# Four-bit feed-forward: Pool's passes over h in quarters of 176 columns, VectorE's sum into the output in one pass over both tiles

## The chip, the cores and the metric

The kernel runs on one core of a Trainium2 chip. The metric is the device time of one execution in microseconds (us), read as the median of the runs; smaller is better. The core has TensorE (matrix products, PE in the profile; its weight loads are PEld), VectorE (DVE), ScalarE (ACT), GpSimd (POOL, called Pool below) and SyncE (SP, which here issues the loads and stores). Each engine works through its own list of instructions in order; they meet through semaphores.

## The reference

A batch of 2 x 2048 rows of 256 numbers goes through four blocks, each added to x behind a layer normalisation: an agent attention, a transformer layer with sixteen heads and eight experts, a selective scan, and a feed-forward whose operands are rounded to four bits. Only the last block is touched:

```python
def fp4_quant_dequant(x):                       # blocks of 16 along the last axis
    scale = jnp.max(jnp.abs(xb), axis=-1, keepdims=True) / 6.0
    scale = jnp.maximum(scale, jnp.float32(1e-12))
    xn = xb / scale
    idx = jnp.searchsorted(_MID, jnp.abs(xn))
    q = _GRID[idx] * jnp.sign(xn) * scale
gate = fp4_linear(x, w_gate)                    # 256 -> 704, x and w both rounded
y = fp4_linear(x, w_up)
h = jax.nn.silu(gate) * y
return fp4_linear(h, w_down)                    # 704 -> 256, h rounded too
x = x + _layernorm(that)
```

## The kernel before, in words

The 4096 rows are 32 tiles of 128 rows (128 partitions); `fp4_ffn` takes two tiles at a time (UT = 2), so 16 units. A unit passes through stages that lie on five engines. `run_stages` writes each engine's list: in step s the engine does, in the order given, its stages, each for the unit s - behind. The order of the work of an engine is thus fixed by hand, and semaphores alone tie the engines together.

What happens to a unit u: TensorE projects (`project`, into ps_p), VectorE adds xm and takes the statistics (`add_xm`), ScalarE normalises into z, VectorE makes x3 (`make_x3`), ScalarE normalises x3 into xf, VectorE rounds xf to four bits (`make_x`, lines 2389 to 2408), Pool takes the rounding constant off again and multiplies by the scale (`scale_x`, L2732 and L2736, into xq). TensorE turns xq (`turn_x`, L2841), ScalarE and VectorE split it in a high and a low part (`copy_x` L2761, `split_xq` L205), and TensorE makes gate and up in 18 products a tile (`gate_up`, L2850). ScalarE brings them into gate, up and sig (`take_gu`), Pool multiplies up by gate (`times_up`, L2715), ScalarE finishes the sigmoid, and Pool multiplies by it into h (`times_sigmoid`, L2725; h is 2 x 704 = 1408 columns a partition). VectorE rounds h (`make_h`): the maximum of each block (L2389), its scale (L2391), the inverse (L2393), the product (L2402), two operations that build the rounding constant (L2404, L2406) and the sum with it (L2408). Pool subtracts the constant (`scale_h`, L2744) and multiplies by the scale into hq (L2750). TensorE turns hq (`turn_h`, L2859) and multiplies by the down weights (`down`, L2867), VectorE takes the statistics (`stats_out`), ScalarE normalises into v (`scale_out`), VectorE adds x3 into o (`make_out`, L2703), and SyncE stores it.

Pool's order in a step: `times_sigmoid` of the unit s - 3, `scale_h` of s - 4, `scale_x` of s - 1, `times_up` of s - 2. Each of the four passes over h goes over two tiles in two halves of 352 columns, so it is four instructions. The x passes are two instructions of 256 columns each.

VectorE's order: `stats_out`, `add_xm`, `stats_x3`, `variances`, `split_xq`, `scales` (four operations on six numbers a partition, L2665 to L2671, called the tiny operations below), `make_h` of s - 4, `make_x3`, `make_x`, `make_out`.

Semaphores that matter: `gu_product` counts the pieces of `times_up`, and `times_sigmoid` waits until all of its unit are there; `gu_used` rises once behind the last piece of `times_sigmoid`, and VectorE's `make_h` waits for it; `h_rounded` rises when L2408 is done and starts the subtraction; `hq_steps` counts the subtracted pieces; `hq_turned` (TensorE) lets Pool write hq again; `hq_ready` rises once behind the last scaled piece; `out_ready` counts finished tiles of the output, for SyncE's store and ScalarE's `scale_out`.

Of the kernel before, what the change touches and what calls it, by code (L numbers as in the profile page):

```python
# [16 lines left out]
ALU = mybir.AluOpType  # L17
# [135 lines left out]
def run_stages(eng, units, *stages, unroll=False, ways=2):  # L153

    stages = [(stage, behind, own[0] if own else units) for stage, behind, *own in stages]

    def step(s, way):
        for stage, behind, count in stages:  # L160
            if not isinstance(s, int) or 0 <= s - behind < count:
                stage(s - behind, (way - behind) % ways)

    starts, ends = [behind for _, behind, _ in stages], [behind + count for _, behind, count in stages]
    if unroll:
        for s in range(min(starts), max(ends)):
            step(s, s % ways)
        return

    first, last = -(-max(starts) // ways) * ways, min(ends) // ways * ways  # L170
    for s in range(min(starts), first):
        step(s, s % ways)
    with eng.Fori(first // ways, last // ways) as i:
        for way in range(ways):
            step(i * ways + way, way)
    for s in range(last, max(ends)):
        step(s, s % ways)


def third_on(unit):  # L180

    return not isinstance(unit, int) or unit >= 2
# [6 lines left out]
def over(ap, shape):  # L189

    return ap.broadcast_to(shape)
# [2187 lines left out]
FP4 = 16  # L2379
FFN = 704  # L2380
HT = -(-FFN // P)
UT = 2
# [29 lines left out]
QUARTERS = 4  # L2412


def quarters(n):

    return [slice(i * n // QUARTERS, (i + 1) * n // QUARTERS) for i in range(QUARTERS)]


def halves(n):  # L2420

    return slice(0, n // 2), slice(n // 2, n)


def in_blocks(ap):

    return ap.rearrange("p (b k) -> p b k", k=FP4)
# [117 lines left out]
def fp4_ffn(nc, io, scratch, out, ident):  # L2545

    with ExitStack() as ctx:
# [9 lines left out]
        def unit_rows(ap, u):  # L2557
            return ap[bass.ds(u * (UT * P), UT * P), :].rearrange("(t p) c -> p t c", p=P)

        def load(sp, u, slot):  # L2560
            sp.dma_start(gated[:, slot, :, :], scratch.gated[:, bass.ds(u * (UT * P), UT * P)].rearrange("(d p) n -> p d n", p=P)).then_inc(in_loaded[slot], 16)
            sp.dma_start(xm[:, slot, :, :], unit_rows(scratch.xm, u)).then_inc(in_loaded[slot], 16)
            sp.dma_start(x2[:, slot, :, :], unit_rows(scratch.x2, u)).then_inc(in_loaded[slot], 16)
# [8 lines left out]
        x3, xf, xq = r.sb("x3", [P, TILES, C]), r.sb("xf", [P, UT, C]), r.sb("xq", [P, UT, C])  # L2572
        x_magic, x_round = r.sb("x_magic", [P, UT, C]), r.sb("x_round", [P, UT, C])
        XB, HB = UT * C // FP4, UT * FFN // FP4
# [6 lines left out]
        v, o = r.sb("v", [P, UT, C]), r.sb("o", [P, 2, UT, C])  # L2581
# [17 lines left out]
        s = {n: r.sem(n) for n in names}  # L2599
# [4 lines left out]
        with nc.Block() as block:  # L2604
            @block.sync
            def _(sp):
                def reload(u, slot):
                    sp.wait_ge(s["x3_ready"], u + 1)
                    load(sp, u + 2, slot)

                def store(u, slot):
                    sp.wait_ge(s["out_ready"], (u + 1) * UT)
                    sp.dma_start(unit_rows(out_rows, u), o[:, slot, :, :]).then_inc(out_stored[slot], 16)

                for slot in range(2):
                    sp.sem_inc(out_stored[slot], 16)
                run_stages(sp, UNITS4, (reload, 0, UNITS4 - 2), (store, 6))
                for slot in range(2):
                    sp.wait_ge(out_stored[slot], (UNITS4 // 2 + 1) * 16)

            @block.vector
            def _(dve):
# [76 lines left out]
                def make_out(u, slot):  # L2699
                    dve.wait_ge(s["o_taken"], (u + 1) * UT)  # L2700
                    dve.wait_ge(out_stored[slot], (u // 2 + 1) * 16)
                    for k in range(UT):
                        dve.tensor_tensor(o[:, slot, k, :], v[:, k, :], x3[:, bass.ds(u * UT + k, 1), :], ALU.add).then_inc(s["out_ready"], 1)  # L2703

                run_stages(dve, UNITS4, (stats_out, 6), (add_xm, 0), (stats_x3, 1), (variances, 0, STEPS4), (split_xq, 2), (scales, 0, STEPS4),
                           (make_h, 4), (make_x3, 0), (make_x, 1), (make_out, 6), unroll=True)

            @block.gpsimd
            def _(pool):
                def times_up(u, slot):  # L2710

                    pool.wait_ge(s["gu_taken"], (u + 1) * UT * 6)
                    for k in range(UT):
                        for f in halves(FFN):
                            pool.tensor_tensor(up[:, slot, k, f], up[:, slot, k, f], gate[:, slot, k, f], ALU.mult).then_inc(s["gu_product"], 1)  # L2715

                def times_sigmoid(u, slot):

                    pool.wait_ge(s["sig_ready"], u + 1)
                    pool.wait_ge(s["gu_product"], (u + 1) * 2 * UT)  # L2720
                    if third_on(u):
                        pool.wait_ge(s["h_rounded"], u - 1)
                    for k in range(UT):
                        for f in halves(FFN):
                            ins = pool.tensor_tensor(h[:, slot, k, f], up[:, slot, k, f], sig[:, slot, k, f], ALU.mult)  # L2725
                    ins.then_inc(s["gu_used"], 1)

                def scale_x(u, slot):

                    pool.wait_ge(s["x_rounded"], u + 1)  # L2730
                    for k in range(UT):
                        pool.tensor_tensor(x_round[:, k, :], x_round[:, k, :], x_magic[:, k, :], ALU.subtract).then_inc(s["q_steps"], 1)  # L2732
                    pool.wait_ge(s["xq_turned"], u)
                    for k in range(UT):
                        pool.wait_ge(s["q_steps"], u * UT + k + 1)
                        ins = pool.tensor_tensor(in_blocks(xq[:, k, :]), in_blocks(x_round[:, k, :]),  # L2736
                                                 over(x_scale[:, k * XB // UT:(k + 1) * XB // UT].unsqueeze(2), [P, XB // UT, FP4]), ALU.mult)
                    ins.then_inc(s["xq_ready"], 1)

                def scale_h(u, slot):  # L2740
                    pool.wait_ge(s["h_rounded"], u + 1)
                    for k in range(UT):
                        for f in halves(FFN):
                            pool.tensor_tensor(h_round[:, k, f], h_round[:, k, f], h_magic[:, k, f], ALU.subtract).then_inc(s["hq_steps"], 1)  # L2744
                    pool.wait_ge(s["hq_turned"], u * UT * 2)
                    for k in range(UT):
                        for i, f in enumerate(halves(FFN)):
                            pool.wait_ge(s["hq_steps"], (u * UT + k) * 2 + i + 1)
                            at, n = k * HB // UT + f.start // FP4, FFN // 2 // FP4
                            ins = pool.tensor_tensor(in_blocks(hq[:, k, f]), in_blocks(h_round[:, k, f]),  # L2750
                                                     over(h_scale[:, at:at + n].unsqueeze(2), [P, n, FP4]), ALU.mult)
                    ins.then_inc(s["hq_ready"], 1)

                run_stages(pool, UNITS4, (times_sigmoid, 3), (scale_h, 4), (scale_x, 1), (times_up, 2))

            @block.scalar
            def _(act):
# [11 lines left out]
                def scale(out, x, n):  # L2769
                    return act.activation(out, x, ACT.Identity, bias=nmr[:, n:n + 1], scale=rstd[:, n:n + 1])  # L2770
# [12 lines left out]

                def scale_out(u, slot):
                    act.wait_ge(s["scale_ready"], u + 7)
                    act.wait_ge(s["out_ready"], u * UT)
                    for k in range(UT):
                        scale(v[:, k, :], ps_o[:, k, :], 2 * UT + k).then_inc(s["o_taken"], 1)

# [26 lines left out]
                def second_tile(stage):  # L2816
                    return lambda u, slot: stage(u, slot, 1)

                act.wait_ge(s["padded"], 3)
                run_stages(act, UNITS4, (copy_x, 2), (all_rstd, 0, STEPS4), (first_tile(take_gu), 2), (scale_y, 0), (scale_x3, 1), (scale_out, 6),  # L2820
                           (first_tile(copy_h), 5), (second_tile(take_gu), 2), (second_tile(copy_h), 5), (sigmoid, 2))

# [117 lines left out]
```

## Time and profile before

| | before |
|---|---|
| median of 3 runs | 3878.36 us (3876.31 to 3887.24) |
| profiled execution | 3878.8 us, span 3877.1 us |
| granted TensorE clock, mean over the span | 0.92 of full |
| busy over the span | PE 3319.7 us, DVE 2915.2, ACT 2051.5, POOL 1173.6 |
| instructions | DVE 4552, POOL 910 |
| the four-bit feed-forward | from about 3457 us to the end |

Times in rows are microseconds from the start of the span, unless a column says ns. A row of a timeline merges instructions of one kind that follow each other: "3.60 ... x4" is the stretch from the first one's start to the last one's end. "L2744" is line 2744 of the kernel. What stands in square brackets is the idle time of the engine before the row and what ended it.

### The profile page before, as it was taken

How to read it: one execution, taken by the hardware profiler on the slowest of the kernel's cores; microseconds unless marked ns; L12 is line 12 of the kernel's file. 1: busy time of each engine (PE TensorE's matmuls, PEld its weight loads, DVE VectorE, ACT ScalarE, POOL GpSimd, SP SyncE). 2: the span in 40 equal slices, each digit the busy share in tenths (PEclk: the TensorE clock that was granted, in tenths of full speed). 3: DMA queues.
4: the chain of work that ended last, by engine and by line, in shares of the span. 5: the costliest groups of instructions: out<-in, count | busy, mean ns of one | idle time of the engine just before them, and what ended most of it. 6: DMA issues, size and time to landing. Idle time of an engine off the chain costs nothing. (4 is left out here: it accounts for less than half of the span.)

```text
span 3877.1 us, 79472 instructions
## 1 busy us (share of the span) xinstructions
PE 3319.7 (86%) x30842; PEld 1891.7 (49%) x30843; DVE 2915.2 (75%) x4552; ACT 2051.5 (53%) x2972; POOL 1173.6 (30%) x910
## 2 busy tenths in 40 slices
PE   4769999999999999969599775988699999847876
PEld 1433333333333333326366553333587787636665
DVE  5659999999999999914444344767599999868986
ACT  0316777777777777753111044666565756325553
POOL 0100000000000000002300171000699999847775
PEclk8969999999999999987799875999899999979998
DMA  1664022130303030033222243333534434221110
GB/s 54 228 173 46 11 42 29 22 48 4 47 5 47 4 47 4 4 106 132 90 65 65 77 134 131 110 121 122 153 111 137 130 108 140 72 72 58 54 35 17
DMA packets 221843, 296.40 MB, mean 76 GB/s; under 512 B 56377, under 2 KB 154946, under 8 KB 219842
## 3 DMA queue, kind: packets, MB, share of 16 engines
q1 hardware_dynamic: 204258, 258.24, 25.1%
q0 software_dynamic: 6144, 17.05, 1.3%
q10 hardware_dynamic: 11120, 16.62, 1.2%
q8 instruction: 228, 3.74, 0.4%
q14 instruction: 93, 0.76, 0.1%
HBM read 174.75 MB, written 116.47 MB: 75 GB/s over the span
## 5 line engine op out<-in xcount | busy, mean ns | idle before, releaser
L921 DVE TENSOR_REDUCE att_maxima<-att_ps_m 128x1 f32<-128x512 f32 x2048 | 1275.4, 682 | 163.5 <-PE att_ps_m L977 158.8
L876 ACT ACTIVATE att_probs<-att_ps_s 128x1024 f32<-128x1024 f32 x1024 | 998.4, 1021 | 382.5 <-PE att_ps_s L992 378.6
L977 PE MATMUL att_ps_m<-att_ks,att_qs 48*128 48x512 f32 x2048 | 743.1, 487 | 72.0 <-DMA att_ks<-scratch_k 29.3
L977 PEld LDWEIGHTS att_ps_m<-att_ks,att_qs 48*128 48x128 f32 x2048 | 299.8, 187 | 758.2 <-DVE att_maxima L921 650.2
L2225 POOL TENSOR_TENSOR ss_ch<-ss_h,ss_c_rep 128x1024 f32<-128x1024 f32 x256 | 602.8, 2443 | 12.8 <-DVE ss_h L2312 12.7
L1003 PE MATMUL att_ps_o<-att_probs,att_vs 128*32 128x512 f32 x4096 | 546.2, 605 | 0.5 <-ACT att_probs L876 0.5
L2344 PE MATMUL ss_ps_u<-ss_diag,ss_dx_t 128*32 128x128 f32 x16384 | 476.3, 275 | 29.1 <-DMA ss_dx_t<-scratch_dx_t 14.6
L2344 PEld LDWEIGHTS ss_ps_u<-ss_diag,ss_dx_t 128*32 128x32 f32 x16384 | 454.8, 111 | 85.6 <-issue 66.9
L992 PE MATMUL att_ps_s<-att_qs,att_ks 50*128 50x512 f32 x2048 | 466.5, 401 | 1.8 <-ACT att_probs L876 0.7
L2264 ACT ACTIVATE ss_decay<-ss_delta,ss_a_neg 128x1024 f32<-128x1024 f32 x256 | 293.8, 1148 | 232.7 <-DVE ss_h L2312 210.1
L2312 DVE TENSOR_TENSOR_SCAN ss_h<-ss_decay,ss_ps_u 128x1024 f32<-128x1024 f32 x128 | 286.7, 2275 | 47.6 <-PE ss_ps_u L2344 38.7
L2312 DVE TENSOR_TENSOR_SCAN ss_h<-ss_decay,ss_carry,ss_ps_u 128x1024 f32<-128x1024 f32 x128 | 293.0, 2333 | 7.8 <-POOL ss_ch L2225 4.5
L992 PEld LDWEIGHTS att_ps_s<-att_qs,att_ks 50*128 50x128 f32 x2048 | 278.8, 186 | 34.1 <-ACT att_probs L876 23.7
L849 POOL TENSOR_TENSOR att_m_parts<-att_m_t,att_m_parts 16x128 fp32r<-16x128 f32 x32 | 14.4, 450 | 737.5 <-ACT att_m_parts L896 737.5
L856 POOL TENSOR_TENSOR att_heads<-att_o_t,att_sums 128x256 f32<-128x256 f32 x32 | 19.9, 622 | 705.1 <-DVE att_sums L936 705.1
L1447 ACT ACTIVATE ex_y<-ex_ps_y,ex_x 128x256 f32<-128x256 f32 x72 | 34.2, 474 | 303.2 <-PE ex_ps_y L1518 303.2
L1651 POOL DMA_INDIRECT mo_back<-scratch_sorted_y,moe_packed x64 | 61.2, 956 | 345.5 <-DMA mo_b_norm<-in_b_norm 318.7
L2026 PE MATMUL si_ps_xz<-si_xn_t,si_w_in 128*128 128x512 f32 x256 | 119.2, 621 | 35.4 <-DMA si_xn_t<-scratch_xn_t 15.9
L1003 PEld LDWEIGHTS att_ps_o<-att_probs,att_vs 128*32 128x32 f32 x4096 | 80.6, 108 | 126.2 <-issue 124.6
L1500 PE MATMUL ex_ps_h<-moe_w_w,ex_x_t 128*128 x288 | 137.2, 599 | 0.4 <-issue 0.4
L2365 PE MATMUL ss_ps_y<-ss_ch,ss_sum_block 128*32 128x512 f32 x1024 | 124.7, 602 | 14.7 <-POOL ss_ch L2225 14.5
L1518 PE MATMUL ex_ps_y<-moe_w_w,ex_hid_t 128*128 x576 | 136.1, 379 | 0.0
(391 smaller groups left out, 4471.9 us busy)
## 6 DMA issues: line engine op xcount, KB each, us to landing
ss_delta<-scratch_delta SPq DMA_DIRECT2D x256, 128.0 KB, 3.1
att_qs<-scratch_q SPq DMA_DIRECT2D x96, 128.0 KB, 10.1
att_ks<-scratch_k SPq DMA_DIRECT2D x96, 128.0 KB, 11.2
ex_x<-scratch_sorted_x SPq DMA_DIRECT2D x72, 132.0 KB, 2.1
scratch_sorted_y<-ex_y SPq DMA_DIRECT2D x72, 128.0 KB, 1.7
scratch_v<-qkv_v_ext SPq DMA_DIRECT2D x8, 1024.0 KB, 4.4
scratch_q<-qkv_parts SPq DMA_DIRECT2D x16, 512.0 KB, 5.3
scratch_k<-qkv_parts SPq DMA_DIRECT2D x16, 512.0 KB, 6.0
```

The lines of the kernel that those rows point to most:

```text
L876: act.activation(probs[:, (2 * n + pair) % 4, :, :], ps_s[pair][:, :, :], ACT.Exp, scale=HD ** -0.5).then_inc(exp_done, 1)
L921: dve.tensor_reduce(maxima[:, j, at:at + 1], ps_m[plan.bank(key)][:, :], AX.X, ALU.max).then_inc(maxed, 1)
L977: pe.matmul(ps_m[plan.bank(key)][:, :], qs[own, s // QC % 2, s % QC, p, t * P:(t + 1) * P], ks[own, s // QC % 2, p, c * GN:(c + 1) * GN], ...
L992: mm = pe.matmul(ps_s[pair][:, e, :], ks[rows_of(e, 0, ROWS), st // QC % 2, pair, kt * P:(kt + 1) * P], qs[rows_of(e, 0, ROWS), st // QC % ...
L1003: mm = pe.matmul(ps_o[h * VW:(h + 1) * VW, :], vs[st // QC % 2][:, kt, h * VW:(h + 1) * VW], probs[:, (2 * n + h // 2) % 4, h % 2, :], sta ...
L1500: mm = pe.matmul(ps_h[slot][:, :], x_t[:, slot, k, :], w1[:, bass.ds(e, 1), k, :].rearrange("p a f -> p (a f)"), start=k == 0, stop=k == K ...
L1518: mm = pe.matmul(ps_y[slot][:, 0, :], hid_t[:, slot, f, :], w2[:, bass.ds(e, 1), f, :].rearrange("p a c -> p (a c)"), start=f == 0, stop=f ...
L2225: pool.tensor_tensor(ch[:, w.n % (CH_GROUPS * DQ), :], h[:, w.n % H_SLOTS, :], c_rep[:, w.ng, :], ALU.mult).then_inc(s["ch_ready"], 1)
L2264: act.activation(decay[:, w.n % DECAYS, :], delta[:, w.delta % DELTAS, :], ACT.Exp, scale=a_neg[:, at:at + 1]).then_inc(s["decay_ready"], 1)
L2312: dve.tensor_tensor_scan(h[:, w.n % H_SLOTS, :], decay[:, w.n % DECAYS, :], ps_u[w.n % U_BANKS][:, :], start, ALU.mult, ALU.add).then_inc( ...
L2344: mm = pe.matmul(ps_u[w.n % U_BANKS][q * DSUB:(q + 1) * DSUB, j * P:(j + 1) * P], dx_t[:, w.part % 2, j, w.dq * DSUB:(w.dq + 1) * DSUB], d ...
L2365: mm = pe.matmul(ps_y[dq * DSUB:(dq + 1) * DSUB, cols], block[:, :], ch[:, group % CH_GROUPS * DQ + dq, cols], start=False, stop=group % N ...
```

## The change

Pool's four passes over h (`times_up`, `times_sigmoid` and both of `scale_h`) go over a tile in four quarters of 176 columns (11 blocks of 16) instead of two halves of 352; the semaphore counts follow. VectorE's `make_out` is one operation over both tiles (512 columns a partition) instead of one a tile, and `out_ready` counts units instead of tiles.

```diff
@@ -2417,11 +2417,6 @@
     return [slice(i * n // QUARTERS, (i + 1) * n // QUARTERS) for i in range(QUARTERS)]
 
 
-def halves(n):
-
-    return slice(0, n // 2), slice(n // 2, n)
-
-
 def in_blocks(ap):
 
     return ap.rearrange("p (b k) -> p b k", k=FP4)
@@ -2609,7 +2604,7 @@
                     load(sp, u + 2, slot)
 
                 def store(u, slot):
-                    sp.wait_ge(s["out_ready"], (u + 1) * UT)
+                    sp.wait_ge(s["out_ready"], u + 1)
                     sp.dma_start(unit_rows(out_rows, u), o[:, slot, :, :]).then_inc(out_stored[slot], 16)
 
                 for slot in range(2):
@@ -2699,8 +2694,7 @@
                 def make_out(u, slot):
                     dve.wait_ge(s["o_taken"], (u + 1) * UT)
                     dve.wait_ge(out_stored[slot], (u // 2 + 1) * 16)
-                    for k in range(UT):
-                        dve.tensor_tensor(o[:, slot, k, :], v[:, k, :], x3[:, bass.ds(u * UT + k, 1), :], ALU.add).then_inc(s["out_ready"], 1)
+                    dve.tensor_tensor(o[:, slot, :, :], v[:, :, :], x3[:, bass.ds(u * UT, UT), :], ALU.add).then_inc(s["out_ready"], 1)
 
                 run_stages(dve, UNITS4, (stats_out, 6), (add_xm, 0), (stats_x3, 1), (variances, 0, STEPS4), (split_xq, 2), (scales, 0, STEPS4),
                            (make_h, 4), (make_x3, 0), (make_x, 1), (make_out, 6), unroll=True)
@@ -2711,17 +2705,17 @@
 
                     pool.wait_ge(s["gu_taken"], (u + 1) * UT * 6)
                     for k in range(UT):
-                        for f in halves(FFN):
+                        for f in quarters(FFN):
                             pool.tensor_tensor(up[:, slot, k, f], up[:, slot, k, f], gate[:, slot, k, f], ALU.mult).then_inc(s["gu_product"], 1)
 
                 def times_sigmoid(u, slot):
 
                     pool.wait_ge(s["sig_ready"], u + 1)
-                    pool.wait_ge(s["gu_product"], (u + 1) * 2 * UT)
+                    pool.wait_ge(s["gu_product"], (u + 1) * QUARTERS * UT)
                     if third_on(u):
                         pool.wait_ge(s["h_rounded"], u - 1)
                     for k in range(UT):
-                        for f in halves(FFN):
+                        for f in quarters(FFN):
                             ins = pool.tensor_tensor(h[:, slot, k, f], up[:, slot, k, f], sig[:, slot, k, f], ALU.mult)
                     ins.then_inc(s["gu_used"], 1)
 
@@ -2740,13 +2734,13 @@
                 def scale_h(u, slot):
                     pool.wait_ge(s["h_rounded"], u + 1)
                     for k in range(UT):
-                        for f in halves(FFN):
+                        for f in quarters(FFN):
                             pool.tensor_tensor(h_round[:, k, f], h_round[:, k, f], h_magic[:, k, f], ALU.subtract).then_inc(s["hq_steps"], 1)
                     pool.wait_ge(s["hq_turned"], u * UT * 2)
                     for k in range(UT):
-                        for i, f in enumerate(halves(FFN)):
-                            pool.wait_ge(s["hq_steps"], (u * UT + k) * 2 + i + 1)
-                            at, n = k * HB // UT + f.start // FP4, FFN // 2 // FP4
+                        for i, f in enumerate(quarters(FFN)):
+                            pool.wait_ge(s["hq_steps"], (u * UT + k) * QUARTERS + i + 1)
+                            at, n = k * HB // UT + f.start // FP4, FFN // QUARTERS // FP4
                             ins = pool.tensor_tensor(in_blocks(hq[:, k, f]), in_blocks(h_round[:, k, f]),
                                                      over(h_scale[:, at:at + n].unsqueeze(2), [P, n, FP4]), ALU.mult)
                     ins.then_inc(s["hq_ready"], 1)
@@ -2783,7 +2777,7 @@
 
                 def scale_out(u, slot):
                     act.wait_ge(s["scale_ready"], u + 7)
-                    act.wait_ge(s["out_ready"], u * UT)
+                    act.wait_ge(s["out_ready"], u)
                     for k in range(UT):
                         scale(v[:, k, :], ps_o[:, k, :], 2 * UT + k).then_inc(s["o_taken"], 1)
```

## Rows read from the trace of the kernel before

**Rows 1.** Busy time by engine: from:to, length, busy (instructions), clock, DMA.

```profile
3507.00:3817.00 310.00, 243.99 (x1127) 203.27 (x1128) 273.90 (x441) 160.43 (x346) 235.98 (x260) 0.93 0.13 44
```

**Rows 2.** Timeline of Pool: start, length, engine, line, operation, count [idle before].

```profile
3507.52 4.58 POOL L2744 TENSOR_TENSOR fp_h_round<-fp_h_round,fp_h_magic 128x352 f32<-128x352 f32 x4 [5.14 <-DVE fp_h_round L2408]
...
3614.24 3.60 POOL L2715 TENSOR_TENSOR fp_up<-fp_up,fp_gate 128x352 f32<-128x352 f32 x4
...
3617.92 3.63 POOL L2725 TENSOR_TENSOR fp_h<-fp_up,fp_sig 128x352 f32<-128x352 f32 x4
...
3626.71 4.11 POOL L2744 TENSOR_TENSOR fp_h_round<-fp_h_round,fp_h_magic 128x352 f32<-128x352 f32 x4 [5.15 <-DVE fp_h_round L2408]
...
3631.26 3.83 POOL L2750 TENSOR_TENSOR fp_hq<-fp_h_round,fp_h_scale 128x352 f32<-128x352 f32 x4 [0.44 <-PE fp_ps_h L2859]
...
3636.79 1.20 POOL L2736 TENSOR_TENSOR fp_xq<-fp_x_round,fp_x_scale 128x256 f32<-128x256 f32 x2
...
3637.94 3.60 POOL L2715 TENSOR_TENSOR fp_up<-fp_up,fp_gate 128x352 f32<-128x352 f32 x4
...
3817.54 3.92 POOL L2744 TENSOR_TENSOR fp_h_round<-fp_h_round,fp_h_magic 128x352 f32<-128x352 f32 x4 [5.16 <-DVE fp_h_round L2408]
```

**Rows 3.** Timeline of VectorE in one step.

```profile
3616.27 0.71 DVE L2665 SCALAR_TENSOR_TENSOR fp_ln_newton<-fp_ln_r 128x6 f32<-128x6 f32 x1
3617.01 0.85 DVE L2667 SCALAR_TENSOR_TENSOR fp_ln_newton<-fp_ln_moments,fp_ln_newton 128x6 f32<-128x6 f32 x1
3617.90 0.17 DVE L2669 SCALAR_TENSOR_TENSOR fp_ln_rstd<-fp_ln_newton,fp_ln_r 128x6 f32<-128x6 f32 x1
3618.10 0.78 DVE L2671 SCALAR_TENSOR_TENSOR fp_ln_nmr<-fp_ln_moments,fp_ln_rstd 128x6 f32<-128x6 f32 x1
3618.80 1.60 DVE L2389 TENSOR_REDUCE fp_h_amax<-fp_h 128x88 f32<-128x1408 f32 x1
...
3621.49 1.62 DVE L2402 TENSOR_TENSOR fp_h_round<-fp_h,fp_h_inv 128x1408 f32<-128x1408 f32 x1
...
3623.15 0.89 DVE L2404 TENSOR_SCALAR fp_h_magic<-fp_h_round 128x1408 int32<-128x1408 int32 x1
...
3625.00 1.63 DVE L2408 SCALAR_TENSOR_TENSOR fp_h_round<-fp_h_round,fp_h_magic 128x1408 f32<-128x1408 f32 x1
...
3634.37 1.88 DVE L2703 TENSOR_TENSOR fp_o<-fp_v,fp_x 128x256 f32<-128x256 f32 x2
```

**Rows 4.** Timeline: VectorE and Pool at one handover.

```profile
3632.93 0.96 POOL L2750 TENSOR_TENSOR fp_hq<-fp_h_round,fp_h_scale 128x352 f32<-128x352 f32 x1
...
3633.28 1.16 DVE L2408 SCALAR_TENSOR_TENSOR fp_x_round<-fp_x_round,fp_x_magic 128x512 f32<-128x512 f32 x1
...
3633.86 1.23 POOL L2750 TENSOR_TENSOR fp_hq<-fp_h_round,fp_h_scale 128x352 f32<-128x352 f32 x1
```

**Rows 5.** Durations in ns, shortest/median/longest, first and last start.

```profile
L2715 POOL TENSOR_TENSOR fp_up<-fp_up,fp_gate x64: 919/931/948, 3476.3 to 3827.0; 128x352 f32<-128x352 f32 x64
...
L2732 POOL TENSOR_TENSOR fp_x_round<-fp_x_round,fp_x_magic x32: 717/724/908, 3455.1 to 3803.2; 128x256 f32<-128x256 f32 x32
...
L2736 POOL TENSOR_TENSOR fp_xq<-fp_x_round,fp_x_scale x32: 612/618/630, 3456.5 to 3804.4; 128x256 f32<-128x256 f32 x32
...
L2750 POOL TENSOR_TENSOR fp_hq<-fp_h_round,fp_h_scale x64: 782/963/1234, 3512.1 to 3858.7; 128x352 f32<-128x352 f32 x64
...
L2225 POOL TENSOR_TENSOR ss_ch<-ss_h,ss_c_rep x256: 2329/2442/2547, 2749.2 to 3376.5; 128x1024 f32<-128x1024 f32 x128
...
L2408 DVE SCALAR_TENSOR_TENSOR fp_x_round<-fp_x_round,fp_x_magic x16: 692/1156/1160, 3454.3 to 3798.9; 128x512 f32<-128x512 f32 x16
```

**Rows 6.** Timeline of TensorE in the same step.

```profile
3614.83 5.31 PE L2833 MATMUL fp_ps_p<-fp_w_out,fp_gated 128*128 128x256 f32 x16
...
3630.27 0.82 PE L2859 MATMUL fp_ps_h<-all_ident,fp_hq 128*128 128x128 f32 x6
```

**Rows 7.** Chain that ended last, in order of time: start, length, what.

```profile
3827.09 0.91 DVE fp_ln_newton L2665
```

## Prediction

> **What bounds the kernel now.** I read the page's slices first, then busy times by stretch, then the timeline of Pool and of VectorE over one step, then the durations of Pool's instructions, then TensorE and the chain of waits. The change touches only the four-bit feed-forward, the last 420 us of the span. In its steady part no engine is full: in the 310 us from 3507 VectorE is busy 273.90, TensorE 243.99, Pool 235.98 [rows 1]. So it is a ring of dependences, to be read from one step. Pool's subtraction pass over h starts at 3507.52 and, thirteen steps later, at 3817.54 [rows 2]: 310.02 / 13 = 23.85 us a step.
>
> The ring of one step, in [rows 2, 3]: Pool leaves xq for `times_up` at 3614.24; TensorE turns xq, it is split, and VectorE issues the first of four tiny normalisation operations at 3616.27; they end at 3618.88; `make_h` runs from 3618.80 to 3626.63; Pool, idle for 5.15 us until then, starts the subtraction at 3626.71, the scaling at 3631.26, then the x passes, and leaves the next xq at 3637.94: 23.70 us later, the period. Pool's `times_up` and `times_sigmoid` (3614.24 to 3621.55) are beside the ring: behind them Pool waits.
>
> A second path is almost as long. TensorE's last turn of the old hq lies at 3630.27 plus 0.82 [rows 6], and Pool's scaling pass waited for it, 0.44 us [rows 2].
>
> **How Pool and VectorE share.** The four tiny operations move six numbers a partition each. One takes 0.17 us, the others 0.71, 0.85 and 0.78 [rows 3]. The slow ones end where an instruction of Pool's ends. In [rows 4] both directions are seen: Pool's piece at 3632.93 ends at 3633.89, VectorE's operation issued at 3633.28 ends 0.55 later at 3634.44, and Pool's piece started at 3633.86 ends 0.65 after that, at 3635.09, in 1.23 us instead of the shortest 0.782 [rows 5]. They take turns, one whole instruction each. So a shorter Pool instruction shortens what one VectorE operation waits; that is what quarters can give.
>
> **Part 1, what a Pool instruction costs.** The shortest durations of the plain form are 717 ns at 256 columns, 919 at 352 and 2329 at 1024 [rows 5]: (919 - 717) / 96 = 2.10 ns a column, (2329 - 919) / 672 = 2.10 as well. At 176 columns that gives 919 - 176 x 2.10 = 549 ns. Starts follow closer than durations: two xq instructions fill 3637.94 - 3636.79 = 1.15 us [rows 2], 0.575 each against a duration of 0.618, so 0.04 is overlapped. Spacing at 352 is then 0.88, at 176 0.51. Two quarters cost 1.02 for 0.88: 0.14 us for every split instruction. For the scaling form 612 ns at 256 and 782 at 352 give 1.77 a column and 470 ns at 176: spacing 0.43 against 0.745, 0.12 a split. A pass has four halves: the three plain passes grow by 0.54 us each, the scaling by 0.5. On the ring stand the subtraction and the scaling: +1.04 us a step. No waiter gains by the finer pieces: `gu_used` and `hq_ready` still rise once, behind the last piece, and the waits on `gu_product` and `hq_steps` ask for the same work as before.
>
> The Trainium skill (GPSIMD Engine Reference, Instruction dispatch) says that each instruction costs the dispatcher one indirect call, "tens of cycles". As an estimate from that page, with 99 cycles at its 1.2 GHz, a split costs at most 0.08 us and the ring would grow by 0.66 instead of 1.04. The fixed part in this trace is larger, 0.14 us from three sizes on one line, and the trace decides.
>
> **Part 2, VectorE's four tiny operations.** With quarters Pool's pieces end each 0.51. From 3616.27 the first operation waits for a boundary (0.05 to 0.5), the next three about 0.5 each, one perhaps slipping in as the one at 3617.90 did. The chain ends at about 3618.4 instead of 3618.88: -0.5 us; bounds -1.0 (the first finds the boundary at once) and 0.
>
> **Part 3, where the longer passes reach.** `times_up` and `times_sigmoid` are beside the ring but grow by 0.54 each. Before, `times_sigmoid` ends at 3617.92 + 3.63 = 3621.55, just where `make_h` issues its first large shared operation (3621.49, 1.62 us, never disturbed) [rows 2, 3]. After, it would end at about 3622.6, and that operation is issued 0.5 earlier, at 3621.0. So about three quarters are still to come. `make_h` then has four large operations in a row that want the shared access (L2402, L2404, L2406, L2408), and a waiting quarter gets its turn between two of them. One turn costs: the quarter ends 0.43 after VectorE's release (0.55 less what an instruction saves that had waited: 0.65 for 0.782 in Pool's case, 0.55 for the shortest 0.692 in VectorE's, [rows 4, 5]), and VectorE's next ends 0.76 behind that (0.89 less 0.13), 1.19 instead of 0.92: +0.27. Three turns: +0.8. If VectorE is earlier still, more quarters are left for it to meet, so the gain of part 2 pays for itself again. Parts 2 and 3 together: 0.8 - 0.5 = +0.3 us; bounds -0.5 (the passes do not meet) and +0.9 (four turns and a gain of only 0.2).
>
> In `make_x`, which runs beside Pool's subtraction and scaling, the number of VectorE operations is the same, so Pool is held as often; VectorE itself ends earlier, which nobody on the ring waits for.
>
> **Part 4, one sum into the output.** Two operations of 256 columns took 1.88 us together at 3634.37, each waiting for a turn [rows 3]; one of 512 waits once for a shorter piece, about 0.45 + 0.55 = 1.0. That takes 0.9 us from VectorE behind `make_x`. It lies beside Pool's x passes; the operation that is next on the ring waits for xq and TensorE, so I cost it at nothing, bounds -0.35 and +0.25 (Pool is held for 512 columns at one time). The store waits for both tiles as before; SP has slack.
>
> **Sum.** 1.04 + 0.3 = +1.34 us a step, 13 steps: +17.4. The tail: in the last steps the tiny operations are on the chain of waits, one of 0.91 at 3827.09 [rows 7]; six such waits (three in that step, three in the next) lose about 0.33 each, -2.0, and the last subtraction and scaling add 1.04: -1.0. Together +16.4. The profiled execution took 3878.8 us (span 3877.1), the median of the runs is 3878.36. 3878.4 + 16.4 = 3895 us.
>
> The Trainium skill (Perfetto Trace Analysis, GPSIMD Instruction) advises to time Pool by start-to-start spacing and not by the reported duration. By durations alone a split would cost 0.18 instead of 0.14 and the ring's passes 1.4 instead of 1.04, and the sum would be some 4.5 us more. The 0.04 of overlap in the rows agrees with the page, so I keep the spacing.
>
> **Rivals.**
> A. The shorter waits win, faster. The mechanism is part 2 alone: every wait of VectorE for Pool is halved. For it: VectorE is the busiest engine, and three of four tiny operations wait. It decides if a split costs under 0.03 us and the longer `times_sigmoid` does not meet `make_h`: then -1.0 + 0.2 = -0.8 a step, 13 x -0.8 - 2 = -12: 3866. Against it: the three sizes on one line. Chance 0.07.
> B. No change that can be seen (under 0.3%, 11.6 us, about what a measurement tells). The passes cost their 1.04, part 2 gives 0.9 back and the collision of part 3 stays away or is spread thinly: +0.2 to +0.7 a step, 3880 to 3887, centre 3883. For it: Pool's piece can start late enough that VectorE issues first. Chance 0.22.
> C. My forecast, +1.0 to +1.7 a step: 3890 to 3900. Chance 0.5.
> D. TensorE's path becomes the later one. With longer idle times before `turn_x` the clock may be low for longer; the granted clock is 0.93 of full in this stretch already [rows 1], and the projection at 3614.83 took 5.31 us [rows 6]. TensorE's turn ends 3631.09 - 3614.24 = 16.9 us into the step; Pool's subtraction, 4.55 + 0.54 behind 12.5 + 0.3, would end at 17.9: 1.0 of room. If it is lost by 1 us in half of the steps: +6.5 on top, 3901; with four turns in part 3, 3906. Chance 0.16.
> E. The merge does harm or good by itself (0.35 a step, 4.5 us): inside the ranges above. Chance that it is all that is seen: 0.05, 3876 to 3881.
>
> **Numbers.** Time 3895. A reaches 3866, B 3880 to 3887, C 3890 to 3900, D 3906. Leaving out A, a part of E and the end of D: 3880 to 3905. Slower by over 0.3% (above 3890): C, D and a little of B, 0.68. Within: B's rest, E, 0.25. Faster: 0.07.
>
> **What would show it.** Pool instructions of 128x176 of about 0.55 us (0.47 scaling) in the quiet tail: part 1. The subtraction and scaling passes together over a microsecond longer: the ring's term. L2402 to L2408 of `make_h` with durations above their 1.62 and 0.89, and quarters of L2725 starting inside them: part 3. The tiny operations at 0.4 to 0.5 us: part 2. The period of L2744's first start at 25.2 instead of 23.85. The forecast is wrong if a quarter takes under 0.46 us, if `times_sigmoid` ends before L2402, or if Pool's wait for TensorE grows.

## The result, and the profile after

The changed kernel takes 3909.4 us (median of 6 runs, 3904.43 to 3914.45), the kernel before 3878.75 us (6 runs): ratio 1.0075, 95% interval 1.0061 to 1.009. It is slower by 31 us, almost twice the 16.4 us that I forecast, and past the end of my range.

Columns as in [rows 1]: busy time by engine in the steady stretch. In the same 310 us Pool is now busy for 251.20 instead of 235.98 [rows 1], and every other engine is busy for less, because fewer steps fit into the stretch.

```profile
3507.00:3817.00 310.00, 233.54 (x1042) 194.03 (x1041) 245.29 (x400) 146.76 (x316) 251.20 (x434) 0.90 0.13 43
```

Pool's timeline answers to [rows 2]: the first and fourteenth subtraction pass, and one whole step.

```profile
3512.91 5.28 POOL L2738 TENSOR_TENSOR fp_h_round<-fp_h_round,fp_h_magic 128x176 f32<-128x176 f32 x8 [1.56 <-DVE fp_h_round L2408]
...
3641.74 6.37 POOL L2738 TENSOR_TENSOR fp_h_round<-fp_h_round,fp_h_magic 128x176 f32<-128x176 f32 x8 [5.08 <-DVE fp_h_round L2408]
...
3654.15 4.16 POOL L2709 TENSOR_TENSOR fp_up<-fp_up,fp_gate 128x176 f32<-128x176 f32 x8
3658.47 4.21 POOL L2719 TENSOR_TENSOR fp_h<-fp_up,fp_sig 128x176 f32<-128x176 f32 x8 [0.16 <-POOL fp_up L2709]
...
3849.18 4.57 POOL L2738 TENSOR_TENSOR fp_h_round<-fp_h_round,fp_h_magic 128x176 f32<-128x176 f32 x8 [5.08 <-DVE fp_h_round L2408]
```

Thirteen steps take 3849.18 - 3512.91 = 336.27 us, 25.87 a step instead of 23.85: +26.25. From the fourteenth pass to the end of the span it is 63.5 us instead of 59.6, +4.0; the first steps add 0.2. Together 30.5, the whole difference of the medians. (The profiled execution is 35.6 us longer; 5 of these lie ahead of Pool's first instruction in the feed-forward, where the change does nothing; single executions of one kernel differ by as much.)

VectorE in the same step, which answers to [rows 3]:

```profile
3656.33 2.00 DVE L2660 SCALAR_TENSOR_TENSOR fp_ln_newton<-fp_ln_r 128x6 f32<-128x6 f32 x1
...
3658.56 0.48 DVE L2664 SCALAR_TENSOR_TENSOR fp_ln_rstd<-fp_ln_newton,fp_ln_r 128x6 f32<-128x6 f32 x1
3659.08 0.48 DVE L2666 SCALAR_TENSOR_TENSOR fp_ln_nmr<-fp_ln_moments,fp_ln_rstd 128x6 f32<-128x6 f32 x1
...
3661.13 0.57 DVE L2391 TENSOR_SCALAR fp_h_scale<-fp_h_amax 128x88 f32<-128x88 f32 x1
...
3662.47 1.69 DVE L2402 TENSOR_TENSOR fp_h_round<-fp_h,fp_h_inv 128x1408 f32<-128x1408 f32 x1
```

The last two tiny operations wait for one quarter each, 0.48 us instead of 0.85, as forecast. The first is the surprise. It is issued at 3656.33, while a quarter of `times_up` runs that ends at 3656.76. Pool's timeline shows the next quarter, which starts all the same:

```profile
3656.72 0.56 POOL L2709 TENSOR_TENSOR fp_up<-fp_up,fp_gate 128x176 f32<-128x176 f32 x1
```

In all, three more quarters start and end, and the operation is let in only at 3658.3, when the pass is over (3654.15 + 4.16 = 3658.31). Three ends of quarters went by before the one that let it in. It moves six numbers a partition and takes 2.00 us. So the chain ends at 3659.56, 5.4 us into the step instead of 4.6, `times_sigmoid` (to 3662.68) and L2402 (3662.47) hardly meet, as before, and the ring is longer at both ends: in the passes on it and in the wait.

Durations, shortest/median/longest in ns, of the changed kernel, beside [rows 5]:

```profile
L2709 POOL TENSOR_TENSOR fp_up<-fp_up,fp_gate x128: 552/558/573, 3481.5 to 3860.8; 128x176 f32<-128x176 f32 x128
L2744 POOL TENSOR_TENSOR fp_hq<-fp_h_round,fp_h_scale x128: 473/482/937, 3518.2 to 3894.5; 128x176 f32<-128x176 f32 x128
```

552 and 473 ns: 549 and 470 were worked out.

### The profile page after: what moved, and what is told of

Its sections match the earlier page's. It is cut to its first block and busy times, and to the rows that moved or that the text cites. A ratio compares the mean times of both kernels' runs of the same rounds, so it can differ in the third digit from the quotient of the medians.

```text
span 3912.7 us, 79760 instructions
## 1 busy us (share of the span) xinstructions
PE 3340.9 (85%) x30842; PEld 1906.5 (49%) x30843; DVE 2892.8 (74%) x4536; ACT 2051.5 (52%) x2972; POOL 1216.3 (31%) x1166
```

## The experiments

All are measured against the kernel before on the same chip. "A row" below is the number of Pool instructions in sequence since Pool last paused (over 0.06 us) or was last held up by VectorE, up to and with the one that runs when the first tiny operation is issued; I counted it in the traces. The longer table stands behind the experiments.

**merge_only.** The kernel before with the sum in one operation.

```diff
 # make_out (and the count of out_ready in its two waits)
-                    for k in range(UT):
-                        dve.tensor_tensor(o[:, slot, k, :], ...)
+                    dve.tensor_tensor(o[:, slot, :, :], v[:, :, :], x3[:, bass.ds(u * UT, UT), :], ALU.add)
```

> The kernel before with VectorE's sum into the output in one operation of 512 columns, Pool's passes left in halves. Theory 1 (the loss is Pool's: extra pieces on the ring and VectorE's first tiny operation waiting behind many of them): 3879 us, within 4 us of before, and the first tiny operation (L2665's counterpart) keeps 0.2 to 0.9 us. Theory 2 (the merged operation holds Pool for longer and is a part of the loss): a step of 24.2 to 24.4 instead of 23.9 and 3884 to 3886 us.

3880.24 us against 3875.6, ratio 1.0019 (1.0004 to 1.0034). The steps are not longer: 23.80 us. From VectorE's first instruction of the feed-forward to the first subtraction pass its profiled execution takes 75.0 us instead of 72.0; but quarters_beside_ring (74.4) and mixed_pieces (77.4) take longer there too, without the merge. So the merge is no part of the loss in the steps; whether it costs 0.2% elsewhere stays open.

**quarters_beside_ring.**

```diff
 # times_up, times_sigmoid (and the count of gu_product)
-                        for f in halves(FFN):
+                        for f in quarters(FFN):
```

> The kernel before with quarters in times_up and times_sigmoid alone, the two passes that Pool has time for; subtraction and scaling stay in halves. Before the first tiny operation Pool then runs about 3 + 4 + 2 + 2 + 4 = 13 to 15 instructions without being held up. Theory 1 (VectorE starves behind a long undisturbed row of Pool instructions, here near the lengths at which it was seen, 14 and more, against 11 and less where it was not): the tiny operation either takes 1.5 to 2 us, a step grows by 0.8 and the time is 3889, or it does not, and the time is 3880 to 3884 because times_sigmoid then reaches into make_h. Theory 2 (short pieces as such take VectorE's turn away, whatever came before): it takes 1.5 to 2 us in every step, 3889 us. Theory 3 (only the length of the passes on the ring counts): 3879.

3878.87 us, ratio 1.0014 (0.9997 to 1.0031), 23.91 us a step. The row is 8 to 11 long, not the 13 to 15 that I had foreseen, so theory 1 is not put to the test here. The first tiny operation takes 0.40 us in the median though the pieces are quarters: theory 2, short pieces as such, falls. And here my forecast for parts 2 and 3 is seen as it was written. VectorE, one step:

```profile
3618.87 0.43 DVE L2667 SCALAR_TENSOR_TENSOR fp_ln_newton<-fp_ln_moments,fp_ln_newton 128x6 f32<-128x6 f32 x1
...
3622.87 1.66 DVE L2402 TENSOR_TENSOR fp_h_round<-fp_h,fp_h_inv 128x1408 f32<-128x1408 f32 x1
3624.57 1.15 DVE L2404 TENSOR_SCALAR fp_h_magic<-fp_h_round 128x1408 int32<-128x1408 int32 x1
3625.74 1.13 DVE L2406 TENSOR_SCALAR fp_h_magic<-fp_h_magic 128x1408 f32<-128x1408 f32 x1
3626.91 1.86 DVE L2408 SCALAR_TENSOR_TENSOR fp_h_round<-fp_h_round,fp_h_magic 128x1408 f32<-128x1408 f32 x1
```

L2404, L2406 and L2408 have 1.15, 1.13 and 1.86 instead of 0.89, 0.89 and 1.63: three turns of about 0.25. In the mean of twelve steps the tiny operations end 0.57 us earlier and the four large ones take 0.73 longer.

**quarters_on_ring.** Quarters in the subtraction and the scaling alone.

```diff
 # scale_h, both passes (and the count of hq_steps)
-                        for f in halves(FFN):
+                        for f in quarters(FFN):
```

> The kernel before with quarters in the subtraction and scaling passes alone; times_up and times_sigmoid stay in halves. Both passes together 1.17 us longer in every step, 13 x 1.17 = 15 us, 3894 us, if nothing else happens (theory 2: the pieces beside the first tiny operation are long, so it waits for one of them, 0.2 to 0.9 us). Theory 1: 8 + 2 + 2 + 2 or 3 undisturbed instructions stand before that operation, it waits until times_up ends, 1.1 to 1.6 us, the ring grows by another 0.3 to 0.7 a step: 3898 to 3903.

3898.66 us, ratio 1.0058 (1.0035 to 1.008); 25.30 us a step, +1.45. The row is 11 to 14. The pieces of `times_up` are as long as before, and yet VectorE is passed over at the end of one and waits for a second, the last of `times_up`, in eight of thirteen steps. Timeline of VectorE in one of them:

```profile
3630.21 1.13 DVE L2665 SCALAR_TENSOR_TENSOR fp_ln_newton<-fp_ln_r 128x6 f32<-128x6 f32 x1
```

**after_wait_before_up.** The changed kernel with a wait on Pool.

```diff
                 def times_up(u, slot):
+                    pool.wait_ge(s["xq_ready"], min(u + 2, UNITS4) if isinstance(u, int) else u + 2)
                     pool.wait_ge(s["gu_taken"], (u + 1) * UT * 6)
```

> The changed kernel with one more wait on Pool: before times_up it waits for its own last xq piece to be complete, so that it comes to times_up with nothing in flight. Theory 1 (what starves VectorE is the long undisturbed row before): four or five pieces stand between the wait and the first tiny operation, it takes at most 0.5 us, the four tiny operations end 0.7 to 1.0 us earlier in the step; times_sigmoid then reaches into make_h as I had forecast, which costs 0.3 to 0.8, and the wait itself 0.1: 0 to 8 us less than the changed kernel, 3901 to 3909. Theory 2 (short pieces as such): the operation still takes 1.5 to 2 us and the time is that of the changed kernel plus 1 us.

3901.66 us, ratio 1.0069 (1.0048 to 1.0089); 25.17 us a step, 0.70 less than the changed kernel. The tiny operations end 1.4 us earlier in the step; half of that goes again into `make_h`, which `times_sigmoid` now meets (0.35), and into Pool's own waits (0.3). In time the gain over the changed kernel (1.0075, 1.0061 to 1.009) is not clear of noise, and the kernel before stays faster. The operation is at 0.155 to 0.406 us in the thirteen steps of the steady part (0.51 and 0.60 in the two steps ahead of it). In one late step no x pass is left, the wait is fulfilled beforehand, and Pool arrives with a row of 20. Timeline of VectorE there:

```profile
3852.38 1.75 DVE L2660 SCALAR_TENSOR_TENSOR fp_ln_newton<-fp_ln_r 128x6 f32<-128x6 f32 x1 [0.61 <-ACT fp_ln_r L2762]
```

Within one kernel, one profile and the same pieces: with the pause at most 0.60, without it 1.75.

**many_x_pieces.** The kernel before, nothing in quarters but the x passes, which have eight pieces of 64 columns each instead of two of 256.

```diff
 # scale_x, both passes
-                    for k in range(UT):
-                        pool.tensor_tensor(x_round[:, k, :], ...)
+                    for k in range(UT):
+                        for f in quarters(C):
+                            pool.tensor_tensor(x_round[:, k, f], ...)
```

> The kernel before, with the two x passes in eight pieces of 64 columns each instead of two of 256; all passes over h stay in halves of 352. Twelve pieces more on the ring at 0.14 us: +1.7 us a step. Theory 1 (VectorE's first tiny operation starves when more than about 12 Pool instructions have run since Pool was last held up or idle; what they are does not matter): 17 to 20 stand before it, it waits for two or three halves of times_up, 1.1 to 1.6 us instead of 0.2 to 0.7, and the ring grows by another 0.8 where it does: 25.9 to 26.4 us a step, about 3904 to 3910. Theory 2 (what counts is how short the pieces are that run when the operation arrives): these are the halves of before, it waits for one: 25.6 us a step, about 3898.

3928.28 us, ratio 1.0113 (1.0079 to 1.0147). That is 49 us more than before, far beyond both theories, which had 3898 to 3910; so the verdict rests on the wait and on the step (26.2 us, where theory 1 had 25.9 to 26.4 and theory 2 25.6), and not on the time. The thirteen steps are 31 us longer, and the start of the feed-forward, up to the first subtraction pass, takes 84.2 us instead of 72.0, which I had not counted; the rest, some 6 us, is within the interval. The row is 17 to 22 and the operation waits to the end of `times_up` in all thirteen steps. The time since the start of the last instruction that was held up is 6.4 to 7.2 us in most of them, less than the 8.5 us with a row of 10 that the kernel before has at 3827.09, where the operation waited for the running instruction alone; so it is the number of instructions, not the time. Against before, in the mean of twelve steps, the end of the tiny operations moves by +0.73 (4.82 to 5.55).

**after_wait_before_hq.** The same kind of wait in the changed kernel, placed ahead of the scaling pass.

```diff
 # scale_h, between the two passes
+                    pool.wait_ge(s["hq_steps"], (u + 1) * UT * QUARTERS)
                     pool.wait_ge(s["hq_turned"], u * UT * 2)
```

> The changed kernel with one more wait on Pool, as in the run with a wait before times_up, but placed before the scaling pass: it waits for its own last subtracted piece. The control for that run. Theory 1 (the row of undisturbed pieces since the last pause counts): 8 + 2 + 2 + 4 = 16 stand between this wait and the first tiny operation, so it starves as in the changed kernel, 1.6 to 2 us; a step of 25.9 to 26.0 us, and the time is that of the changed kernel plus 1 to 2 us. Theory 2 (any pause of Pool in a step cures it): at most 0.5 us, a step of 25.2 to 25.3, 8 us less than the changed kernel.

3909.87 us, ratio 1.0085 (1.0057 to 1.0113); the changed kernel had 1.0075. In nine steps the row is 15 to 17 and the operation takes 1.69 to 2.06; in four consecutive steps VectorE's own turns came later, the row is 13 or 14 and it takes 0.15 to 0.45. In four of the nine the row begins at the wait itself; in the others VectorE held Pool up shortly behind it. One step of each kind, from the timeline:

```profile
3537.64 1.98 DVE L2660 SCALAR_TENSOR_TENSOR fp_ln_newton<-fp_ln_r 128x6 f32<-128x6 f32 x1
...
3666.07 0.16 DVE L2660 SCALAR_TENSOR_TENSOR fp_ln_newton<-fp_ln_r 128x6 f32<-128x6 f32 x1
```

A pause as such does not bring VectorE's turn back; one shortly before does.

**whole_tiles_on_ring** and **whole_tiles_ring_and_x.** The other direction: subtraction and scaling in whole tiles of 704 columns, and in the second also each x pass as one instruction.

```diff
 # scale_h, the subtraction; the scaling likewise
-                        for f in halves(FFN):
-                            pool.tensor_tensor(h_round[:, k, f], ...)
+                        pool.tensor_tensor(h_round[:, k, :], ...)
 # the second version, scale_x, the subtraction; the scaling likewise
-                    for k in range(UT):
-                        pool.tensor_tensor(x_round[:, k, :], ...)
+                    pool.tensor_tensor(x_round[:, :, :], ...)
```

> The kernel before with the subtraction and scaling passes in whole tiles of 704 columns, two instructions a pass instead of four; times_up and times_sigmoid stay in halves. The other way from the change. Fixed cost: four pieces less on the ring, 4 x 0.14 = 0.56 us less a step, 13 x 0.56 = 7 us less than before. If Pool is also held up less often (VectorE gets four turns in make_x instead of seven) up to 1.0 less a step; against it VectorE waits 1.3 to 1.6 us a turn, its rounding of x may end behind the scaling pass, and TensorE's turn of hq ends at 16.9 us of the step in every second one, which bounds the gain near 0.4 there. 3864 to 3876 with before at 3876; if make_x becomes late, 3880.

> As the one before, and the two x passes as one instruction of 512 columns each: two pieces less, another 0.28 us a step, 13 x 0.28 = 3.6 us. 3860 to 3872 with before at 3876.

3884.97 and 3884.54 us against 3879.11, ratios 1.0017 (0.9998 to 1.0036) and 1.0007 (0.9989 to 1.0024): no gain. 13 steps take 310.18 and 310.49 us. This is a miss: 3860 to 3876 was expected. Pool's passes are shorter, but it then waits for the rounding of x, because each large operation of VectorE now takes 1.5 us or more with its wait for a whole tile. In the second version the first tiny operation also starts 0.6 us later in the step (2.9 us behind the start of `times_up` instead of 2.3). Timelines of the first, Pool and VectorE:

```profile
3645.98 3.36 POOL L2748 TENSOR_TENSOR fp_hq<-fp_h_round,fp_h_scale 128x704 f32<-128x704 f32 x2
3650.42 1.70 POOL L2732 TENSOR_TENSOR fp_x_round<-fp_x_round,fp_x_magic 128x256 f32<-128x256 f32 x2 [1.09 <-DVE fp_x_round L2408]
...
3644.84 1.72 DVE L2402 TENSOR_TENSOR fp_x_round<-fp_xf,fp_x_inv 128x512 f32<-128x512 f32 x1
3646.59 1.50 DVE L2404 TENSOR_SCALAR fp_x_magic<-fp_x_round 128x512 int32<-128x512 int32 x1
```

**mixed_pieces.** A version that the runs pointed to.

```diff
 # times_up; gu_product counts QUARTERS + 1 a unit
-                        for f in halves(FFN):
+                        for f in quarters(FFN) if k else (slice(0, FFN),):
```

> A version built from what the runs showed: the kernel before, with times_up as one piece of 704 columns (first tile, when VectorE wants nothing shared) and four quarters (second tile, when its tiny operations come); all other passes in halves, so no piece more on the ring and the row before the tiny operations stays under ten. By the turns as measured: the four tiny operations end at 3.3 to 3.9 us of the step instead of 4.8, one turn of a half lies inside make_h (+0.4 to 0.5) and the scale operation waits up to 0.5: make_h ends 0.3 to 0.7 us earlier, a step of 23.2 to 23.6 us instead of 23.85, 3867 to 3873 with before at 3876. Rival: what the tiny operations gain is lost in make_h once more, as in the run with quarters beside the ring: 23.9 us a step and no difference; or TensorE's turn of hq at 16.9 us holds the scaling pass, and only every second step gains: 3873.

3884.54 us against 3883.93, ratio 0.9999 (0.9986 to 1.0011). The tiny operations end 0.7 us earlier, the subtraction starts 0.18 earlier, and the step is 23.77 us: 1 us in thirteen steps. In three steps of twelve TensorE's turn of hq ended at 18 us behind the start of `times_up`, and the step took 24.2 to 24.75. The first rival came nearest: of the 0.7 us that the tiny operations gain, 0.5 are lost again in `make_h`. No version beat the kernel before.

| kernel | row | first tiny operation, shortest/median/longest ns | us a step |
|---|---|---|---|
| before | 5 to 10 | 156/700/948 | 23.85 |
| quarters_beside_ring | 8 to 11 | 157/404/641 | 23.91 |
| quarters_on_ring | 11 to 14 | 154/1128/1589 | 25.30 |
| changed | 14 to 18 | 1535/1706/2157 | 25.87 |
| after_wait_before_up | 4 to 5 | 155/206/406 | 25.17 |
| after_wait_before_hq | 13 to 17 | 154/1686/2056 | 25.71 |
| many_x_pieces | 17 to 22 | 965/1131/1585 | 26.2 |

## Why the prediction was wrong

**What bounds the kernel** held: the ring of the step, with Pool's subtraction and scaling on it and its other two passes beside it. quarters_beside_ring and quarters_on_ring show the two halves apart.

**Part 1** held: a quarter of 549 and 470 ns was worked out, 552 and 473 measured, and both passes on the ring grew by 1.17 us (mean of twelve steps) for 1.04. The fixed cost of about 0.14 us an instruction, from three sizes on one line, was good at 176 columns, below all sizes that the trace of before had. The price from the Trainium skill (GPSIMD Engine Reference, Instruction dispatch), "tens of cycles", would have been too low: at most 0.66 us for the two passes by my estimate, and 1.17 measured.

**Part 2 is the step that failed.** I took it from [rows 4] that the two take turns, one whole instruction each, and so gave each tiny operation one quarter to wait for: -0.5 us. The chain ends 0.56 us later instead, since the first operation is passed over at the ends of two to four quarters in every step. In the whole trace of the kernel before no VectorE operation that waits for Pool comes behind a row of more than ten, and I read as a rule what held in that condition. The change itself took the kernel out of it: with eight pieces a pass the row grows from 5 to 10 to 14 to 18. This is worth 1.06 us a step against the forecast.

**Part 3** was right as a mechanism and did not come to pass in the changed kernel, because the starved operation holds `make_h` back until `times_sigmoid` is over: +0.35 us was left of it (0.28 of this is L2391, 0.57 us where it had 0.27 or so) for +0.8. Where VectorE is not starved it is there, 0.73 for 0.8 (quarters_beside_ring), and pays away the whole gain of part 2.

**Part 4** held in the steps: 23.80 us with the merge alone.

**The tail**: -1.0 was forecast, +4.0 came. The chain that ended last, in order of time:

```profile
3858.83 2.62 DVE fp_ln_newton L2660
...
3875.35 3.56 POOL fp_hq L2744 x8
...
3879.00 1.63 DVE fp_h_amax L2389
```

The operation that was to save 0.33 takes 2.62 instead of 0.91 [rows 7], behind a row of 19. And two subtraction and scaling passes lie on the chain where I counted one: `make_h` of the last unit waits at 3879.00 until the scaling of the unit before is done.

The sum: 1.17 + 0.56 + 0.35 - 0.07 (x passes) = 2.01 us a step for 1.34. Of the 14 us that the forecast lacks, the steps have 8.8 and the tail 5.0. That the change came out slower, as forecast, was no luck, for part 1 alone does that; but part 3 was forecast 0.45 a step too high, and this hid a part of the error of part 2. Rivals A and B are contradicted: of the 0.9 us that B has part 2 give back nothing came, and even where VectorE is not starved it was 0.57. Rival D was not needed: Pool never waited for TensorE in the changed kernel. Nor was it rival E, for the merge leaves the steps as they were.

**What the cause is.** Shown: VectorE is passed over when a long row of Pool instructions stands before it. With rows up to 12 it waits for the end of the running instruction, or for the one behind it where it comes in the last 0.1 us; with 15 and more it always waits to the end of the pass; 13 and 14 went both ways. The end of the pass is no accident: there Pool waits for its own last product before `times_sigmoid` and pauses for 0.08 to 0.43 us (0.16 at 3658.47), and every operation that was passed over behind a row of 13 or more got in at this pause. A pause of Pool shortly before the operation keeps it from being passed over, one 16 instructions earlier does not; neither the size of the pieces nor the time since the last pause or hold decides. Only argued: why. The Trainium skill (GPSIMD Engine Reference, Instruction dispatch) says that each of Pool's eight cores starts the next instruction as soon as its own share of the last is done, with nothing to keep them together. Cores that drift apart over a long row would leave no instant at which all are between two instructions, and a pause or a hold would bring them together again. The runs agree with that; no row shows a single core. The Trainium skill (SBUF — State Buffer, Summary: rules for kernel authors) lets the second of the two engines to issue wait "until the first finishes". That holds behind short rows here; behind long ones the operation waited for up to six instructions, and the measurement decides.

## What to carry to other kernels

Price a split of a Pool pass at about 0.14 us a piece and ask whether the pass is on the path; then count how many Pool instructions run without a pause before a VectorE operation that takes turns with Pool, and if it is many, try one wait of Pool ahead of the place where VectorE must get in. Here that wait took 0.70 us off a step of the changed kernel, but no gain in time that is clear of noise, and it did not make the split worth while. Before halving the pieces for the sake of one waiter, look at what the longer pass reaches next: what the tiny operations gained was paid back in `make_h` by turns. And a rule of sharing read from one trace holds for the state of the queues in that trace; say which state, and whether the change leaves it.

## What the runs showed of the hardware

- A VectorE operation can be passed over at the ends of two to five of Pool's quarters, or of one or two of its halves, before it gets in (2.00 us for an operation that takes 0.17 alone; 2.62 in the tail). With up to 12 Pool instructions since the last pause or hold it was never so, other than where the running one had 0.1 us or less left; with 13 or 14 it went both ways, and with 15 and more it was always so.
- One wait of Pool on its own last instruction, four to five instructions before, brings the same operation back to at most 0.41 us in the steady steps; the same wait 16 instructions before leaves it at 1.69 to 2.06 in nine steps of thirteen.
- Where the two take turns, each turn of a 128x176 piece between two large VectorE operations costs VectorE about 0.25 us (1.15, 1.13 and 1.86 us for 0.89, 0.89 and 1.63 in quarters_beside_ring).
- The shortest time of Pool's float32 subtraction of two tensors is close to linear in the columns: 307 ns at 64, 548 at 176, 717 at 256, 919 at 352, 1671 at 704, and 2329 at 1024 (a product there). From start to start that is about 0.14 us and 2.1 ns a column. Where one input is broadcast over blocks of 16: 282, 473, 612, 782 and 1377 ns from 64 to 704 columns.
